# A cross-attention and expert kernel whose first tile phase takes the rows of five rounds in place of six

## The chip, the cores and the metric

One Trainium2 chip, one of its cores. The metric is the time of one execution on the device in microseconds (us); lower is better.

## The reference

The input x is 32 batches of 128 tokens with 128 features. First comes cross-attention with 16 heads of 8 features, then a layer of experts in which each token goes to its top 2 of 8:

```python
x = x + xattn(layernorm(x), ctx)          # q = x Wq', k and v = ctx Wkv', softmax over 128 keys, Wc'
xf = layernorm(x)
logits = xf @ router_w.T                  # 8 experts
top_vals, top_idx = top_k(logits, 2)
probs = softmax(top_vals)
for e in range(8):
    w = sum(where(top_idx == e, probs, 0))
    h = gelu(xf @ w1[e].T + b1[e])        # 512 hidden features, exact gelu
    out += w * (h @ w2[e].T + b2[e])
x = x + out
```

The 4096 tokens give 8192 rows, one for each token and choice.

## The kernel before

The program has two parts. The first is attention with routing, in slots s = 0 to 36; the second is a loop over 71 tiles of 128 rows.

**Attention.** In slot s the engines work on different steps of different batches. TensorE (PE) makes the scores of batch s, whose maxima DVE takes (`take_max`), and the exponent scores of batch s-3; ACT takes the exponentials; PE attends, transposes and projects batches s-4 and s-5. From slot 32 on there is no new batch, and the slots are shorter. `normalise` is DVE's step on which the transposes of a batch wait.

**Routing.** Four batches make a round; there are eight rounds, r = 0 to 7. Round r is routed in slots 9+4r and after (`routing(s, lag)`): DVE finds the two experts of each token (`top_of`, `mark_equal`, `mark_number`, `first_number`, `choose`, `pick`), sums them (`sum_round`, `carry_on`), PE makes the ranks (`rank`), and DVE turns these into row numbers (`row_ranks`, `row_terms`, `row_numbers`, `row_indices`). The two shares of a token come from the gap of its logits: POOL scales it (`scale_gap`), ACT or POOL takes the exponential (`share_ratio`), DVE finishes (`share_sum`, `share_first`, `share_second`). The normalised rows are made from POOL's `row_scale` and copied for the second choice (`copy_rows`). Then POOL sends them: `send_next` issues one indirect DMA for one batch and one choice, 128 rows, to a table in DRAM (`dispatch_d`) that has a region for each expert. A round has eight sends. Rounds 0 to 4 are sent in the slots by the plan `SENDS` (one, two, three and two sends, four to seven slots after the round begins), where `pace` may hold a send back until the exponentials are that far; round 5 by `SENDS_LAST` in the last three slots; round 6 after the last slot, in one go; round 7, which `route_last` routes on DVE after the last slot, between tiles 8 and 29, every third tile. Three buffers hold the rounds' rows.

**The table.** A tile needs the number of its expert and its first row. DVE works these out on one partition, in chains of small operations that each wait for the one before (`link`). `table_first` (three parts, in slots 33, 34 and 35) does it for the first `FIRST` = 40 tiles, which are filled from rounds 0 to 5 alone (6 x 4 x 128 x 2 rows are 48 tiles, less one for each expert's remainder); `table_second` (ten parts, behind tiles 6 to 15) for the other 31, when all counts are known. The engines load eight tiles' values into registers at a time (`table_values`, at tiles 8, 16 and so on).

**Tiles.** SP loads the expert's w1 (`load_w1`, ring of 6) and the rows (`load_tile`, ring of 12, which waits for the store of the tile 12 earlier). PE transposes the rows (`turn_tile`), ACT copies them (`copy_xg`), PE makes the hidden layer (`up`, line 1235), DVE adds the bias (`add_bias`, line 1768), ACT applies gelu, PE makes the output (`down`, line 1244), DVE adds the bias (`sum_y`), ACT multiplies by the share (`gate_y`), and POOL stores the rows by an indirect DMA (`store_tile`, lines 791 and 792). On each engine `between(t)` puts the late routing work behind the work of tile t. SP waits for the sends of rounds 3 to 5 before tile 0 and for those of rounds 5 to 7 before tile 40; it holds back w1 and rows alike. From tile 58 on ACT loads results of the first six rounds back (`load_found`), DVE adds them to x, and SP stores the output.

```python
            sp.wait_ge(sexp_done, UNITS * FIRST_BATCHES)
            for r in range(FIRST_ROUNDS - RR, FIRST_ROUNDS):
                rows_gone(sp, r)
```

Of the kernel before, what the change touches and what calls it, by code (L numbers as in the profile page):

```python
# [16 lines left out]
P = 128  # L17
# [28 lines left out]
SENDS_LAST = {0: 3, 1: 3, 2: 2}  # L46
# [6 lines left out]
FIRST_ROUNDS = 6  # L53
FIRST_BATCHES = FIRST_ROUNDS * GB
FIRST = FIRST_BATCHES * SEQ * TOPK // P - EXPERTS
REST = TILES - FIRST
OLD_TILES = FIRST + EXPERTS + 7
FIRST_GROUPS = FIRST_BATCHES // GB
# [5 lines left out]
PADS_AT = 24  # L64
LAST_SENDS_AT = 8
# [12 lines left out]
TABLE_STEPS = FIRST_STEPS + 30  # L78
# [14 lines left out]
def xattn_ffn(nc, x, ctx_t, mask, mask_t, wq_t, wkv_t, wc_t, router_t, w1_t, b1, w2_t, b2, out):  # L93
    stack = ExitStack()
    with stack:
# [77 lines left out]
        tile_no_i = sb("tile_no_i", [1, FIRST], I32)  # L173
# [18 lines left out]
        def carve(region):  # L192
            at = [0]

            def take(words):
# [9 lines left out]
        lone = carve(take(2 * TOKENS // P + FIRST + 2 * TILES + 8 * EXPERTS + 2 * EXPERTS * (TOKENS // P) + 12 * EXPERTS + 1  # L205
                          + 2 * max(FIRST * EXPERTS, REST * 2 * EXPERTS) + 2 * FIRST)[0:1])
        tile_lim, tile_no = lone(2 * TOKENS // P), lone(FIRST)
# [9 lines left out]
        expert_f, start_f = lone(FIRST), lone(FIRST)  # L217
# [14 lines left out]
        first_total_ps, total_ps = feed[:, GT - EXPERTS:GT], tail[:, GT - EXPERTS:GT]  # L232
        rank_ps = [(tail if r == ROUND - 1 else feed)[:, 0:GB * EXPERTS] for r in range(ROUND)]
# [180 lines left out]
        def _(sp):  # L414
# [115 lines left out]
            sp.wait_ge(sexp_done, UNITS * FIRST_BATCHES)  # L530
# [42 lines left out]
        def _(pool):  # L573
# [76 lines left out]
            def constants():  # L650
# [4 lines left out]
                nc.gpsimd.iota(tile_no_i[:], [[1, FIRST]], base=0, channel_multiplier=0).then_inc(iotas_made, 1)  # L655
# [69 lines left out]
            for s in range(LAST_SLOT + 1):  # L725
# [27 lines left out]
                if r is not None:  # L753
                    scale_gap(r)
                    if r >= FIRST_ROUNDS:
                        share_ratio(r)
                n = 0
                for lag, count in SENDS.items():
                    r = routing(s, 3 + lag)
                    if r is not None and r < FIRST_ROUNDS - 1:  # L760
                        for _ in range(count):
                            n += 1
                            if n > 1:
                                pace(s, n)
                            send_next(r)
                if s - LAST_SLOT + len(SENDS_LAST) > 0:
                    for _ in range(SENDS_LAST[s - LAST_SLOT + len(SENDS_LAST) - 1]):
                        send_next(FIRST_ROUNDS - 1)
# [35 lines left out]
        def _(act):  # L804
# [113 lines left out]
            for s in range(LAST_SLOT + 1):  # L918
# [43 lines left out]
                if r is not None and r < FIRST_ROUNDS:  # L962
                    share_ratio(r)
# [49 lines left out]
        def _(pe):  # L1013
# [139 lines left out]
            for s in range(LAST_SLOT + 1):  # L1153
# [19 lines left out]
                if r is not None:  # L1173
# [5 lines left out]
                    elif r == FIRST_ROUNDS - 1:  # L1179
                        pe.wait_ge(v_copied, GROUPS)  # L1180
# [97 lines left out]
        def _(dve):  # L1278
# [234 lines left out]
            def table_first(part):  # L1513
# [16 lines left out]
                if part == 2:  # L1530
                    link(nc.vector.tensor_scalar(steps_at[:, 0:EXPERTS], whole, -float(P), float(REGION), ALU.mult, ALU.add))
                    link(nc.vector.tensor_tensor(first(passed), spread(tile_no, EXPERTS), by_tile(ends[1][:, 0:EXPERTS], FIRST), ALU.is_ge))
                    link(nc.vector.tensor_reduce(expert_f, first(passed), AX.X, ALU.add))
                    link(nc.vector.tensor_copy(expert_of[:, 0:FIRST], expert_f))
                    link(nc.vector.tensor_tensor(first(passed2), first(passed), by_tile(steps_at[:, 0:EXPERTS], FIRST), ALU.mult))
                    link(nc.vector.tensor_reduce(start_f, first(passed2), AX.X, ALU.add))
# [297 lines left out]
```

## Time and profile before

| what | value |
|---|---|
| time, median of 3 runs | 385.14 us |
| time, lowest and highest | 384.53, 386.89 us |
| span of the profiled execution, first to last instruction | 383.3 us |
| busy: PE, DVE, ACT, POOL | 81%, 67%, 61%, 63% of the span |
| DMA, mean over the span | 164 GB/s |

The profiled execution is shown by its span; its own time outside the profiler's span isn't given. The median of the runs is 1.8 us above the span. Busy shares are means over stages that differ: attention runs to about 212 us, the tiles from about 221 to 370, and the last results after that.

### The profile page before, as it was taken

The page shows a single profiled execution, that of the slowest core. Times are in us where ns is not written, and L with a number is a line of the kernel's source. Part 1 is how long each engine was busy: PE and PEld are TensorE (multiplying, and loading weights), DVE is VectorE, ACT ScalarE, POOL GpSimd, SP SyncE. Part 2 cuts the span into 40 slices and gives each one's busy share as a digit, 9 for nine tenths or more (in the row PEclk, how much of TensorE's full clock was granted, in tenths as well). Part 3 has the DMA queues.
Part 4 walks back from the last instruction along what each step waited for, and adds up shares of the span by engine and source line. Part 5 has one row for each costly group of instructions (what it writes and reads, how often), then busy time and mean ns, then how long its engine had stood idle before and what let it go on. Part 6 is the DMA issues. An engine that isn't in the chain of part 4 may idle for free.

```text
span 383.3 us, 11559 instructions
## 1 busy us (share of the span) xinstructions
PE 309.2 (81%) x3720; PEld 251.8 (66%) x3720; DVE 255.3 (67%) x750; ACT 232.6 (61%) x566; POOL 241.7 (63%) x387
## 2 busy tenths in 40 slices
PE   1633878998997979797988089999999999999930
PEld 0211546666666657475765079889999999998930
DVE  7406678889788889788868826785545554556752
ACT  1311366879787878877788037556666666666520
POOL 7796335352487786858486786577877666665550
PEclk9999989999999999999999559999999999999995
DMA  5589454566474463442110386575986766669846
GB/s 152 93 212 232 130 138 114 145 111 175 124 201 129 146 170 101 130 130 58 36 54 31 96 262 185 167 223 163 275 239 196 232 202 208 204 172 353 271 119 192
DMA packets 61850, 62.95 MB, mean 164 GB/s; under 512 B 14109, under 2 KB 46260, under 8 KB 61632
## 3 DMA queue, kind: packets, MB, share of 16 engines
q1 hardware_dynamic: 55168, 50.34, 48.6%
q0 software_dynamic: 4320, 8.47, 6.4%
q10 hardware_dynamic: 2304, 3.41, 2.8%
q8 instruction: 32, 0.52, 0.6%
q14 instruction: 26, 0.21, 0.2%
HBM read 37.65 MB, written 11.88 MB: 129 GB/s over the span
## 4 chain that ended last, share of the span: by engine, by line
PE 45%; POOL 21%; issue 14%; DVE 7%; DMA 5%; SPq 4%; ACT 2%; DVEq 0%; POOLq 0%; ACTq 0%
PE sexp L1244 16%; PE smax L1235 15%; POOL dispatch_d L706 10%; PE smax L1040 3%; SPq L443 3%; DVE shift L1315 2%; PE tail L1084 2%; POOL rstd L666 2%; POOL qpart L619 2%; DMA stacks<-result_d 1%; DMA kmask<-mask_dram 1%; POOL shift L626 1%; PE feed L1031 1%; PE feed L1016 1%; POOL xq L614 1%
## 5 line engine op out<-in xcount | busy, mean ns | idle before, releaser
L1315 DVE TENSOR_REDUCE shift<-smax 128x4 f32<-128x512 f32 x128 | 87.0, 684 | 35.8 <-PE smax L1040 34.8
L792 POOL DMA_INDIRECT result_d<-y_out,stacks x71 | 70.7, 995 | 31.3 <-issue 29.5
L706 POOL DMA_INDIRECT dispatch_d<-rows_out,row_i x64 | 63.5, 993 | 34.2 <-DVE rows_out L1444 16.8
L871 ACT ACTIVATE probs<-sexp 128x512 f32<-128x512 f32 x128 | 74.2, 592 | 10.1 <-PE sexp L1048 9.1
L1235 PE MATMUL smax<-probs,w_ring 128*128 128x128 f32 x568 | 77.8, 281 | 1.6 <-ACT probs L978 1.0
L1244 PE MATMUL sexp<-w_sb,probs 128*128 x568 | 77.0, 279 | 2.6 <-ACT probs L982 2.4
L1768 DVE TENSOR_TENSOR probs<-smax,b_cols 128x512 f32<-128x512 f32 x71 | 49.1, 691 | 42.4 <-PE smax L1235 38.5
L1244 PEld LDWEIGHTS sexp<-w_sb,probs 128*128 128x128 f32 x568 | 69.8, 194 | 5.0 <-issue 4.9
L1235 PEld LDWEIGHTS smax<-probs,w_ring 128*128 128x128 f32 x568 | 70.7, 196 | 3.3 <-issue 2.9
L982 ACT ACTIVATE probs<-probs 128x512 f32<-128x512 f32 x71 | 44.8, 631 | 37.6 <-DVE probs L1768 37.5
L1040 PE MATMUL smax<-stacks 64*128 64x128 bf16 x512 | 47.9, 225 | 12.9 <-DMA stacks<-kpart 7.0
L1040 PEld LDWEIGHTS smax<-stacks 64*128 64x128 bf16 x512 | 29.3, 97 | 36.6 <-DVE shift L1315 16.6
L1048 PE MATMUL sexp<-stacks 64*128 64x128 bf16 x512 | 45.9, 219 | 0.0
L1775 DVE TENSOR_TENSOR probs<-sexp,b_sb 128x128 f32<-128x128 f32 x71 | 20.6, 291 | 21.8 <-PE sexp L1244 21.8
L1084 PE MATMUL tail<-probs,values 128*32 128x128 f32 x1024 | 34.6, 276 | 0.3 <-ACT probs L871 0.3
L987 ACT ACTIVATE y_out<-probs,stacks 128x128 f32<-128x128 f32 x71 | 28.3, 399 | 4.2 <-DVE probs L1775 4.1
L1048 PEld LDWEIGHTS sexp<-stacks 64*128 64x128 bf16 x512 | 28.0, 94 | 0.9 <-issue 0.2
L626 POOL TENSOR_TENSOR shift<-shift 128x16 f32<-128x16 f32 x32 | 7.0, 218 | 33.8 <-DVE shift L1315 33.4
L1084 PEld LDWEIGHTS tail<-probs,values 128*32 128x32 f32 x1024 | 26.0, 109 | 3.3 <-ACT probs L871 0.5
L791 POOL TENSOR_TENSOR wait_taker<-zero 128x1 f32<-128x1 f32 x71 | 14.2, 200 | 14.5 <-ACT y_out L987 14.0
L978 ACT ACTIVATE probs<-prep 128x128 f32<-128x128 f32 x36 | 9.9, 275 | 16.6 <-PE prep L1226 16.6
L1226 PE MATMUL prep<-ident_wide,stacks 128*128 128x128 f32 x36 | 10.1, 282 | 9.1 <-DMA stacks<-dispatch_d 9.1
(215 smaller groups left out, 511.4 us busy)
## 6 DMA issues: line engine op xcount, KB each, us to landing
w_ring<-w_t_dram SPq DMA_DIRECT2D x71, 256.0 KB, 3.6
stacks<-kpart SPq DMA_DIRECT2D x48, 128.0 KB
stacks<-qpart SPq DMA_DIRECT2D x48, 128.0 KB
stacks<-dispatch_d SPq DMA_DIRECT2D x71, 65.0 KB, 3.5
stacks<-result_d ACTq DMA_DIRECT2D x12, 256.0 KB, 4.4
ctx<-ctx_t_dram SPq DMA_DIRECT2D x8, 256.0 KB, 3.7
w_sb<-w_t_dram SPq DMA_DIRECT2D x8, 256.0 KB, 3.4
out_dram<-xw SPq DMA_DIRECT2D x8, 256.0 KB, 3.3
```

Source lines behind the costliest of these rows:

```text
L706: nc.gpsimd.indirect_dma_start(out=dispatch_d, out_offset=bass.IndirectOffsetOnAxis(ap=row_i[r % RR][:, k, b:b + 1], axis=0), in_=rows_out ...
L792: nc.gpsimd.indirect_dma_start(out=result_d, out_offset=bass.IndirectOffsetOnAxis(ap=xg[r][:, D + 1:D + 2].bitcast(U32), axis=0), in_=y_ou ...
L871: nc.scalar.activation(dst, sexp[hp][:], ACT.Exp).then_inc(exp_done, 1)
L982: nc.scalar.activation(hidden[i], biased[i], ACT.Gelu).then_inc(gelu_done, 1)
L987: nc.scalar.activation(y_out[r][:], y_sum[i], ACT.Copy, scale=xg[r][:, D:D + 1]).then_inc(y_gated, 1)
L1040: return nc.tensor.matmul(smax[hp][:, i, :], qstack[g][rows, 4 * m + i, ks], kstack[g][rows, 4 * m + i, ks], start=True, stop=True)
L1048: return nc.tensor.matmul(sexp[hp][:, i, :], kstack[g][rows, 4 * m + i, ks], qstack[g][rows, 4 * m + i, ks], start=True, stop=True)
L1084: last = nc.tensor.matmul(tail[32 * j:32 * (j + 1), c * SEQ:(c + 1) * SEQ], values[n // GB % 2][:, n % GB, h, :], probs[n % 2][:, h * SEQ: ...
L1235: last = nc.tensor.matmul(up_ps[i][:, c * P:(c + 1) * P], w1_ring[t % WRING][:, c * P:(c + 1) * P], xg_t[i], start=True, stop=True)
L1244: last = nc.tensor.matmul(down_ps[i], hidden[i][:, c * P:(c + 1) * P], w2_sb[:].rearrange("p e c d -> p (e c d)")[:, bass.ds(e * FF + c * ...
L1315: nc.vector.tensor_reduce(shift4[n % 2][:, hp, 0, 4 * m:4 * m + 4], smax[hp][:], AX.X, ALU.max, negate=True).then_inc(max_taken, 1)
L1768: nc.vector.tensor_tensor(biased[i].rearrange("p (c t) -> p c t", c=FC), up_ps[i].rearrange("p (c t) -> p c t", c=FC), bias, ALU.add).then ...
```

## The change

The first phase of tiles takes the rows of five rounds: `FIRST_ROUNDS` is 5 and `FIRST` 32. The constants `OLD_ROUNDS` and `OLD_BATCHES` keep the value of six for what still depends on it (the tiles below 55, and the results that ACT loads early). The first table is made two slots earlier, in slots 31 to 33, and PE's total for it in slot 30. Round 5 is now sent by `SENDS`, in slots 33 to 36. Round 6 is sent twice before the tiles and then once behind each of tiles 0 to 5; round 7 behind tiles 9, 11 and so on to 23. `route_last` is cut into three pieces behind tiles 0, 1 and 2, and the steps after it move with it: rows at tile 3, ranks at 5, row numbers at 6, shares at 7, POOL's gap and ratio at tile 3. The second table now serves 39 tiles; it also needs the tiles filled by six rounds, from a second total (`old_total_ps`), and has eleven parts, behind tiles 8 to 18. The pads go out from tile 16.

```diff
-SENDS_LAST = {0: 3, 1: 3, 2: 2}
-FIRST_ROUNDS = 6
+FIRST_ROUNDS = 5
+OLD_ROUNDS = 6
-PADS_AT = 24
-LAST_SENDS_AT = 8
+PADS_AT = 16
+SENDS_BEFORE = 2
+LAST_SENDS_AT = 9
+TABLE_AT = 8
...
 # SP, before tile 0
-            sp.wait_ge(sexp_done, UNITS * FIRST_BATCHES)
+            sp.wait_ge(sexp_done, UNITS * OLD_BATCHES)
...
 # POOL
-                    if r is not None and r < FIRST_ROUNDS - 1:
+                    if r is not None and r < OLD_ROUNDS:
                         for _ in range(count):
...
-                if s - LAST_SLOT + len(SENDS_LAST) > 0:
-                    for _ in range(SENDS_LAST[s - LAST_SLOT + len(SENDS_LAST) - 1]):
-                        send_next(FIRST_ROUNDS - 1)
...
-            for _ in range(TOPK * GB):
-                send_next(FIRST_ROUNDS)
+            for _ in range(SENDS_BEFORE):
+                send_next(ROUND - 2)
             row_scale(ROUND - 1)
             place_rows(ROUND - 1)
-            scale_gap(ROUND - 1)
-            share_ratio(ROUND - 1)
             def between(t):
-                n, off = divmod(t - LAST_SENDS_AT, 3)
+                if t < TOPK * GB - SENDS_BEFORE:
+                    send_next(ROUND - 2)
+                if t == 3:
+                    scale_gap(ROUND - 1)
+                    share_ratio(ROUND - 1)
+                n, off = divmod(t - LAST_SENDS_AT, 2)
                 if off == 0 and 0 <= n < TOPK * GB:
                     send_next(ROUND - 1)
...
 # PE, rank of a round in its slot
                     if r == FIRST_ROUNDS:
                         pe.wait_ge(table_steps, 1)
-                    elif r == FIRST_ROUNDS - 1:
-                        pe.wait_ge(v_copied, GROUPS)
+                    elif r > FIRST_ROUNDS:
+                        routed(pe, r - 1, RANKS_STEP)
...
-                if s == ROUTE_AT + GB * FIRST_ROUNDS:
+                if s == ROUTE_AT + GB * FIRST_ROUNDS + 1:
                     pe.wait_ge(carried, FIRST_ROUNDS)
-                    routed(pe, FIRST_ROUNDS - 1, RANKS_STEP)
+                    pe.wait_ge(v_copied, GROUPS)
...
 # PE, between(t)
-                if t == 1:
+                if t == 4:
                     rank(ROUND - 1)
-                if t == 4:
+                if t == TABLE_AT - 1:
                     pe.wait_ge(carried, ROUND)
                     routed(pe, ROUND - 1, RANKS_STEP)
+                    nc.tensor.matmul(old_total_ps, ones_b[:], carry[:, OLD_ROUNDS, :], start=True, stop=True)
...
 # DVE
-                late = r is not None and r < FIRST_ROUNDS - 1
+                late = r is not None and r < OLD_ROUNDS
...
-                if s == LAST_SLOT - 4:
-                    dve.wait_ge(sexp_done, UNITS * FIRST_BATCHES)
+                if s == BATCH - 2:
+                    dve.wait_ge(sexp_done, UNITS * OLD_BATCHES)
...
-                if LAST_SLOT - 3 <= s < LAST_SLOT:
-                    table_first(s - LAST_SLOT + 3)
+                if BATCH - 1 <= s < BATCH + 2:
+                    table_first(s - BATCH + 1)
...
             def between(t):
                 r = ROUND - 1
-                if t == 1:
+                if t < 3:
+                    route_last(r, t)
+                if t == 3:
                     norm_rows(r)
-                if t == 2:
+                if t == 5:
                     row_ranks(r)
                     row_terms(r)
-                if t == 3:
+                if t == 6:
                     row_numbers(r)
                     row_indices(r)
-                if t == 4:
+                if t == 7:
                     share_sum(r)
                     share_first(r)
                     share_second(r)
-                if 6 <= t < 16:
-                    table_second(t - 6)
+                if 0 <= t - TABLE_AT < 11:
+                    table_second(t - TABLE_AT)
...
-            route_last(ROUND - 1)
```

## Rows read from the trace of the kernel before

**Rows 1.** Chain that ended last, around the seam (start us, us, what).
```profile
215.22 3.15 DMA dispatch_d<-rows_out,row_i
...
218.95 1.92 DMA stacks<-dispatch_d
```

**Rows 2.** Two stretches: us, busy (x count) by engine, TensorE clock, DMA share, GB/s.
```profile
211.00:212.00 1.00, 0.80 (x4) 0.53 (x4) 0.92 (x3) 0.11 (x2) 1.00 (x1) 0.83 0.20 67
...
228.50:229.00 0.50, 0.50 (x9) 0.50 (x8) 0.17 (x1) 0.00 (x0) 0.42 (x4) 0.77 0.73 233
```

**Rows 3.** Timeline of PE: start us, us, engine, line, operation.
```profile
211.47 0.47 PE L1115 MATMUL prep<-wc_wide,y_t 128*128 128x136 f32 x2
...
228.66 1.17 PE L1235 MATMUL smax<-probs,w_ring 128*128 128x128 f32 x8
...
289.61 1.06 PE L1235 MATMUL smax<-probs,w_ring 128*128 128x128 f32 x8
```

**Rows 4.** Timeline of DVE, attention's last slots and the seam.
```profile
199.70 0.66 DVE L1432 TENSOR_SCALAR index<-ratio 128x4 f32<-128x4 f32 x1
...
201.35 0.30 DVE L1330 BATCH_NORM_STATS2 stats<-xw 128x6 f32<-128x128 f32 x1
...
203.11 0.26 DVE L1320 RECIPROCAL denom<-heads 128x16 f32<-128x16 f32 x1 [0.69 <-PE heads L1100]
...
207.12 0.15 DVE L1510 COPY stacks<-stacks 1x2 f32<-1x2 f32 x1
...
208.53 0.16 DVE L1529 SCALAR_TENSOR_TENSOR stacks<-stacks 1x8 f32<-1x8 f32 x1
...
215.34 0.28 DVE L1330 BATCH_NORM_STATS2 stats<-xw 128x6 f32<-128x128 f32 x1
...
219.17 0.17 DVE L1402 TENSOR_TENSOR carry<-carry,round_sum 128x8 bf16<-128x8 bf16 x1
```

**Rows 5.** Timeline of POOL from round 5's sends to the first store.
```profile
204.35 1.05 POOL L706 DMA_INDIRECT dispatch_d<-rows_out,row_i  x1 [0.61 <-issue]
...
216.20 0.64 POOL L683 COPY rows_out<-rows_out 128x512 f32<-128x512 f32 x1
217.64 0.99 POOL L706 DMA_INDIRECT dispatch_d<-rows_out,row_i  x1 [0.81 <-POOL rows_out L683]
...
227.48 1.05 POOL L666 TENSOR_TENSOR rstd<-var_eps,minus_half 128x4 f32<-128x4 f32 x1
...
229.03 0.19 POOL L689 TENSOR_TENSOR scaled_gap<-gap,rstd 128x4 f32<-128x4 f32 x1
...
230.27 0.19 POOL L791 TENSOR_TENSOR wait_taker<-zero 128x1 f32<-128x1 f32 x1
```

**Rows 6.** Timeline of POOL in the tile phase, and its last send.
```profile
261.37 0.96 POOL L706 DMA_INDIRECT dispatch_d<-rows_out,row_i  x1 [0.30 <-issue]
...
263.73 0.23 POOL L791 TENSOR_TENSOR wait_taker<-zero 128x1 f32<-128x1 f32 x1
264.43 0.99 POOL L792 DMA_INDIRECT result_d<-y_out,stacks  x1 [0.47 <-issue]
...
291.20 0.96 POOL L706 DMA_INDIRECT dispatch_d<-rows_out,row_i  x1 [0.30 <-issue]
```

**Rows 7.** Timeline of SP's queue: the first loads after its wait at tile 40.
```profile
297.56 0.33 SPq L520 DMA_DIRECT2D w_ring<-w_t_dram  x1
298.07 0.33 SPq L514 DMA_DIRECT2D stacks<-dispatch_d  x1
```

**Rows 8.** DMA issues on the page: operation, count, KB, median us to landing.
```profile
w_ring<-w_t_dram SPq DMA_DIRECT2D x71, 256.0 KB, 3.6
...
stacks<-dispatch_d SPq DMA_DIRECT2D x71, 65.0 KB, 3.5
```

**Rows 9.** A DVE table operation and the POOL send beside it, by timeline.
```profile
254.20 0.66 DVE L1741 TENSOR_TENSOR stacks<-stacks 1x496 f32<-1x496 f32 x1
...
254.29 1.41 POOL L706 DMA_INDIRECT dispatch_d<-rows_out,row_i  x1 [0.30 <-ACT y_out L987]
```

More of the change, by code:

```diff
@@ L77 @@
 PADS_STEP = FIRST_STEPS + 2
-TABLE_STEPS = FIRST_STEPS + 30
+TABLE_STEPS = FIRST_STEPS + 33
 def bf16_parts(value):
@@ L232, in xattn_ffn @@
         first_total_ps, total_ps = feed[:, GT - EXPERTS:GT], tail[:, GT - EXPERTS:GT]
+        old_total_ps = tail[:, GT - 2 * EXPERTS:GT - EXPERTS]
         rank_ps = [(tail if r == ROUND - 1 else feed)[:, 0:GB * EXPERTS] for r in range(ROUND)]
@@ L961, in _ @@
                 r = routing(s, 3)
-                if r is not None and r < FIRST_ROUNDS:
+                if r is not None and r < OLD_ROUNDS:
                     share_ratio(r)
@@ L1635, in _ @@
                     row_numbers(r)
-                if r is not None and r >= FIRST_ROUNDS - 1:
+                if r is not None and r >= OLD_ROUNDS:
                     row_indices(r)
@@ L1656, in _, with route_last @@
                         row_moments(3)
-            def route_last(r):
-                row_stats2(BATCH - 1)
-                top_of(r, 0)
-                row_moments2(BATCH - 1)
-                mark_equal(r, 0)
-                row_var2(r)
-                mark_number(r, 0)
-                first_number(r, 0)
-                choose(r, 0)
-                mask_first(r)
-                top_of(r, 1)
-                mark_equal(r, 1)
-                mark_number(r, 1)
-                first_number(r, 1)
-                choose(r, 1)
-                pick(r)
-                top_gap(r)
-                sum_round(r)
-                carry_on(r)
+            def route_last(r, part):
+                if part == 0:
+                    row_stats2(BATCH - 1)
+                    top_of(r, 0)
+                    row_moments2(BATCH - 1)
+                    mark_equal(r, 0)
+                    row_var2(r)
+                    mark_number(r, 0)
+                if part == 1:
+                    first_number(r, 0)
+                    choose(r, 0)
+                    mask_first(r)
+                    top_of(r, 1)
+                    mark_equal(r, 1)
+                    mark_number(r, 1)
+                if part == 2:
+                    first_number(r, 1)
+                    choose(r, 1)
+                    pick(r)
+                    top_gap(r)
+                    sum_round(r)
+                    carry_on(r)
             def between(t):
                 r = ROUND - 1
-                if t == 1:
+                if t < 3:
+                    route_last(r, t)
+                if t == 3:
                     norm_rows(r)
-                if t == 2:
+                if t == 5:
                     row_ranks(r)
                     row_terms(r)
-                if t == 3:
+                if t == 6:
                     row_numbers(r)
                     row_indices(r)
-                if t == 4:
+                if t == 7:
                     share_sum(r)
@@ L1712, in table_second @@
                     link(nc.vector.tensor_tensor(count, last_row[0:1, :], first_row[0:1, :], ALU.subtract))
-                if part == 1:
+                if part in (1, 2):
+                    if part == 2:
+                        link(nc.vector.tensor_copy(count, old_total_ps[0:1, :]))
                     link(nc.vector.tensor_tensor(over[:, :, 0, :], spread(count, TOKENS // P),
@@ L1716, in table_second @@
                                                  ALU.is_gt))
-                    link(nc.vector.tensor_reduce(ceil_new, over[:, :, 0, :], AX.X, ALU.add))
+                    link(nc.vector.tensor_reduce((ceil_new, floor_ceil[:, :, 0])[part - 1], over[:, :, 0, :], AX.X, ALU.add))
+                if part == 3:
                     link(nc.vector.tensor_tensor(tiles_of[:, 0:EXPERTS], floor_ceil[:, :, 0], done, ALU.subtract))
-                if part == 2:
                     link(nc.vector.tensor_tensor(tiles_of[:, EXPERTS:], ceil_new, floor_ceil[:, :, 0], ALU.subtract))
@@ L1724, in table_second @@
                                                         in1=first_row[0:1, :], op0=ALU.mult, op1=ALU.add))
-                if part == 3:
+                if part == 4:
                     link(nc.vector.memset(first_at[:, 2 * EXPERTS:], float(EXPERTS * REGION)))
```

45 lines of the change are left out of this document (23 added, 22 removed).

## The prediction

> **What bounds the kernel now.** I read the chain that ended last first. At the seam between attention and tiles it runs through POOL's sends of round 5, the landing of the last one (215.22 + 3.15 = 218.37) and the load of tile 0 (218.95, landed 220.87) [rows 1]. The timeline of PE shows what waits on it: attention's last matmul ends at 211.94, and tile 2's up matmuls start only at 228.66 [rows 3]. The table of stretches adds that TensorE's granted clock falls from 2.4 to 1.2 GHz inside 211 to 212 us, after slots in which PE was partly idle, and is back within 228.5 to 229.0 [rows 2]. From tile 2 to tile 32 PE takes 60.95 us, 2.03 per tile, with DVE's table work in it [rows 3]; from there on the chain is nearly all PE. So a gain must come from the seam, and every later wait of PE counts against it. The change pays for an earlier start with a nearer second deadline: the last round's rows must have landed before tile 32, where they now have until tile 40.
>
> **The seam.** Tile 0 now needs rounds 0 to 4 only, whose sends go out in slots 29 to 32, before the first row of round 5's here (204.35) [rows 5]. What is late next is the table. Its first part on DVE moves from slot 33's end to slot 31's; DVE idles there for normalise, and PE's rank of round 5, which now waits for the first table step, still comes before the shift it would wait for anyway, so I cost slot 31 at nothing. In slot 32 round 5's share work and two constants (199.70 to 201.35, 1.65) leave and the second part (207.12 to 208.69, 1.57) comes in. In slot 33 DVE worked 1.07 us, 201.35 to 202.42, and idled 0.69 before normalise at 203.11 [rows 4]; with the share work, about 1.0 more, round 5's shares are ready at about 203.3 and normalise slips by 0.4 at most. Slots 34 and 35 lose two parts; attention ends at 211.9 plus or minus 1.
> The last table part then ends at about 206.7 (normalise 203.6 to 204.1, and about 2.6, an estimate: it is the longest part). SP needs at most 5.4 us from there to the load (derived below), so tile 0 lands between 212.3 and 214.0. Before, 7.8 us passed from the landing at 220.87 [rows 1] to 228.66, at half clock and with route_last off DVE's path. With the clock fallen likewise, tile 2 starts at 211.9 + 0.3 + 7.8 = 220.0, against 228.66: 8.7 us earlier. If the clock stays up some 2 us more is won; that is one end, the later landing (+1.8) the other. I take the row that exists: half clock.
>
> **DVE after the seam.** route_last (215.34 to 219.34, 4.0 us) [rows 4] goes in three pieces of 1.2 to 1.5 behind tiles 0, 1 and 2. The first lies in the start-up and is free; the others exceed what DVE has free in a tile by 0.2 to 0.5 each, less at half clock. The table of the rest grows: two more operations for the old total, eleven parts for ten, 624 elements for 496 in the four operations over tiles (0.66 each [rows 9], so 0.17 more each), and its longest part now falls in tile 16, where DVE also reloads its registers. I put all this at 1.5 us of PE's time, between 0.5 and 3. The new wait is at tile 7: share_sum of the last round waits for POOL's ratio, with add_bias of tile 8 queued behind it, and PE's down behind that. Tile 8 comes at 220.0 + 6 x 2.03 = 232.2; POOL makes the ratio at about 234.3 (next part); so 1 to 2 us. PE's own path to tile 32: 220.0 + 60.95 + 1.5 + 1.5 = 283.9.
>
> **POOL and the second deadline.** This is the term that decides. Before, from 204.35 POOL works without a break to 216.84: eight sends, place_rows, gap, ratio, copy_rows, 12.49 us [rows 5]. Now the first send can go at 203.6 (shares at 203.3), and row_scale with its offset, which used POOL's idle before, lies inside: 1.3 plus a gap of 0.2, so 203.6 + 12.5 + 1.5 = 217.6. As before, 0.8 pass to round 6's first send: 218.4. Eight of them took 9.84 (217.64 to 227.48), so two take 2.5; row_scale and place_rows 1.55 (227.48 to 229.03) [rows 5]: store 0 at 222.4, where before it was at 230.27. Its tile would have allowed it some 3 us earlier: POOL starts in debt.
> Then six pairs of store and send, each 263.73 - (261.37 - 0.30) = 2.66 [rows 6], 16.0; gap and ratio at tile 3, 1.24 (229.03 to 230.27) [rows 5]; stores 6 to 8 at 2.66 - 1.26 = 1.40, 4.2; seven times two stores and a send, 4.06, 28.4; store 23 and the last send, 2.66. Sum: 222.4 + 16.0 + 1.2 + 4.2 + 28.4 + 2.7 = 274.9 for the end of the last send. PE gives POOL 2.03 per tile, so the debt is hardly paid off before tile 24, and POOL sets this time, not PE.
> Before, the last send ended at 292.16 and SP issued the first load behind its wait at 297.56 [rows 6, 7]: 5.4 us for landing and two register loads. So 280.3 for w1 and 280.8 for the tile; they land 3.6 and 3.5 later in the median [rows 8], 1.9 in an empty queue [rows 1]: 283.9 and 282.7 to 284.3. With about 0.8 for turn and copy tile 32's matmuls start between 283.9 and 285.1, where PE could have started at 283.9. Two chains that end so close, both uncertain, give a little more than either: 284.7. Before it was 289.61 [rows 3]. So of 8.7 us 4.9 are left.
>
> A busy time of POOL would have given another answer: 0.96 for a send where the spacing is 1.26. The Trainium skill (Perfetto Trace Analysis, GPSIMD Instruction) says to time GpSimd by the start-to-start spacing of its instructions and not by the reported duration. The rows agree, with a gap of 0.30 before the send; by durations the fourteen sends behind store 0 alone would come out 4.2 us shorter.
>
> **The rest.** The number of tiles is 71 in both, the register reloads fall on the same tiles, the result loads still begin at tile 58, the tail is the same. Pads go out at tiles 16 to 23 in place of 24 to 31, beside POOL's debt: load 16 waits for store 4, at about 236, landed near 240, and is due at tile 15's transpose, near 247. No cost. The span of 383.3 would become 378.4. The profiled execution is shown by its span alone; the median of the runs is 1.8 above it, which I keep: 385.14 - 4.9 = 380.2.
>
> **Rivals.**
> 1. POOL doesn't bind: the shares come earlier, or its debt is repaid while PE waits on DVE, so that tile 32 finds its rows. For it: PE's own waits at tiles 7 and 16 give POOL time. Against it: POOL is in debt from store 0 on. PE's path alone is 283.9, without the wait at tile 7 282.3, with full clock 280.3: gains of 5.7 to 9.3, 376 to 379.5. Chance 0.15.
> 2. POOL falls further behind, and the change turns slower. Mechanism: a store that follows a store doesn't always take 1.40; at 264.43 a gap of 0.47 stood in it [rows 6], 0.31 more than the 0.16 which the pair has. On 24 stores that is 7.4 us: last send 282.3, tile 32 at about 291.5 to 292.1, 2 us later than before, 387.3. It decides from 4.9 us of additional POOL time on. Against it: the gap stood there once where POOL was behind, and is usual only where it waits. Chance 0.06.
> 3. DVE and POOL get in each other's way. One send took 1.41 in place of 0.96, beside a DVE operation with two inputs of SBUF [rows 9]. If all fourteen sends behind store 0 did, it is 14 x 0.45 = 6.3 us, 1.4 more than the gain: 386.5. The change puts six of them beside route_last. Seven of the eight in the tiles before did not show it, so one or two of these is in my range. Chance 0.05.
> The Trainium skill (SBUF — State Buffer, Who interferes with whom) has such a rule: a DVE instruction with two SBUF inputs holds the read port that GpSimd needs, and one in a 2-port mode both, for the whole instruction. By that rule sends and stores beside the last round's work would be late as in rival 3; the one row agrees, the others leave it open.
> 4. PE's path is longer than mine: the wait at tile 7 spreads (POOL makes the ratio later) and the pieces of route_last each stop PE. Up to 3 us on top: tile 32 at 287 to 288, 383. Chance 0.14.
>
> **How the numbers follow.** The forecast, 378.3 to 382.3 around 380.2, has 0.60; rival 1 0.15, rival 4 0.14, rivals 2 and 3 together 0.11. A measurement of this kernel can tell about 1% from no change, 3.85 us: faster means below 381.3, slower above 389.0. Of the forecast's own chance 0.43 lies below 381.3, with rival 1 0.58, and a little of rival 4: 0.60. Slower by over 1% needs 4 us more than rivals 2 and 3 give in the mean: 0.05. The rest is 0.35. The range runs from 377 (half of rival 1 left out) to 385 (rivals 2 and 3 left out).
>
> **What would show it.** Right: tile 0's load lands near 213 and tile 2 starts near 220; the clock falls near 212 as before; the first send of round 5 near 203.6; store 0 near 222.4; the last send ends near 275 at store 23, with no gap between POOL's stores and sends until then; SP's queue is empty for some microseconds before tile 32, and PE idles there for 1 to 3 us; DVE waits at tile 7 for the ratio. Wrong: a PE wait of 5 us or more at tile 32, a wait for a y_sent before it, tile 2 later than 222, or no wait at tile 32 at all.

## The result and the profile after

The changed kernel takes 392.6 us (median of 4 runs, 391.9 to 394.5) where the kernel before takes 384.9 beside it: ratio 1.0202, 95% interval 1.0165 to 1.0238. The forecast was 380.2, in a range from 377 to 385. The change makes the kernel 2% slower. Every ratio below leaves out single executions that ran slower than the others of their kernel, so it needn't be the quotient of the two medians. The span of the profiled execution is 390.2 us, against 383.3.

The page of the changed kernel: span, busy time, and the chain that ended last.

```profile
span 390.2 us, 11564 instructions
...
PE 309.4 (79%) x3721; PEld 252.5 (65%) x3721; DVE 254.5 (65%) x753; ACT 231.7 (59%) x566; POOL 243.3 (62%) x387
...
PE 37%; POOL 24%; issue 17%; DVE 8%; SPq 4%; DVEq 4%; DMA 3%; ACT 2%; POOLq 0%; ACTq 0%
```

PE is busy as long as before (309 us) and stands still for 7 us more. New in the chain is DVEq, 4% of the span, where the kernel before had 0%: DVE's sequencer, doing something that is no computation. The seam first, since that was the aim. Timelines of PE and POOL of the changed kernel, to be read against [rows 3] and [rows 5]:

```profile
213.93 0.45 PE L1230 MATMUL prep<-ident_wide,stacks 128*128 128x128 f32 x1 [3.62 <-DMA stacks<-dispatch_d]
216.30 2.05 PE L1239 MATMUL smax<-probs,w_ring 128*128 128x128 f32 x8 [1.93 <-issue]
...
221.95 1.06 PE L1239 MATMUL smax<-probs,w_ring 128*128 128x128 f32 x8
...
288.81 1.06 PE L1239 MATMUL smax<-probs,w_ring 128*128 128x128 f32 x8
...
293.22 1.13 PE L1239 MATMUL smax<-probs,w_ring 128*128 128x128 f32 x8 [1.44 <-issue]
```

```profile
202.01 0.99 POOL L710 DMA_INDIRECT dispatch_d<-rows_out,row_i  x1 [2.24 <-DVE rows_out L1449]
...
223.07 0.19 POOL L795 TENSOR_TENSOR wait_taker<-zero 128x1 f32<-128x1 f32 x1 [1.51 <-ACT y_out L991]
...
278.36 0.97 POOL L710 DMA_INDIRECT dispatch_d<-rows_out,row_i  x1 [0.30 <-issue]
```

Tile 2 starts at 221.95, 6.7 us earlier than before. Tile 32 starts at 288.81, 0.8 earlier. After that the kernel only loses. PE's first matmuls on tile 0 show the sign of the cause: 1.93 us between the turned tile and them, with nothing in the profile that released them. What the sequencers do there stands in the rows of line 409, `table_values`, which reads eight tiles' numbers from SBUF into registers. First the changed kernel (engine, operation, count, then shortest, median and longest in ns), then the kernel before, where the same line is 405:

```profile
L409 SPq TENSOR_LOAD <-stacks x18: 1467/1712/1947, 204.6 to 347.0; - x18
L409 DVEq TENSOR_LOAD <-stacks x9: 1658/1881/2181, 212.7 to 357.0; - x9
L409 PEldq TENSOR_LOAD <-stacks x9: 1957/2028/2592, 213.9 to 358.6; - x9
```

```profile
L405 SPq TENSOR_LOAD <-stacks x18: 522/1227/1802, 213.3 to 341.0; - x18
L405 DVEq TENSOR_LOAD <-stacks x9: 594/604/1058, 219.2 to 351.6; - x9
L405 PEldq TENSOR_LOAD <-stacks x9: 587/632/1072, 221.0 to 353.1; - x9
```

There are as many loads as before, of the same size, at the same tiles, and each takes in the median 1.88 us on DVE where it took 0.60, and 2.03 on PE where it took 0.63. (These rows carry a q behind the engine's name: the profile doesn't count them as busy, and most views leave them out.) The chain of the changed kernel shows that they aren't hidden; at tile 24 and at tile 32:

```profile
272.31 0.29 DVE probs L1787
272.60 1.74 DVEq L409
...
274.56 0.70 DVE probs L1780
...
275.39 1.13 PE smax L1239 x8
...
289.41 1.61 DVEq L409
...
291.24 0.70 DVE probs L1780
```

DVE finishes a tile, reads its registers, and only then adds the bias that frees the buffer in which PE makes a later tile. The start of `add_bias` by DVE's timeline gives the sum of it:

| add_bias of tile | before | changed | difference |
|---|---|---|---|
| 2 | 230.06 | 223.77 | -6.3 |
| 32 | 290.81 | 291.24 | +0.4 |
| 39 | 304.26 | 305.87 | +1.6 |
| 40 | 306.15 | 308.98 | +2.8 |
| 58 | 341.07 | 346.49 | +5.4 |
| 70, the last | 365.61 | 372.94 | +7.3 |

From tile 39 to 70, where the two programs do the same work, the changed kernel still loses 5.7 us, and it loses nearly all of them at tiles 40, 48, 56 and 64, where the registers are read again.

**What the change did to these loads.** The table of experts, `expert_of`, lies in one long row of 4-byte words, in the buffer `stacks`, behind the row `tile_no`. (The extract of the diff in The change leaves this edit out.) In the kernel before `tile_no` has `FIRST` = 40 words; in the changed one `MOST` = max(32, 39) = 39. So `expert_of` starts at word 9855 of `stacks` in place of 9856, and each group of eight starts at an odd word in place of a multiple of eight. `start_of`, which lies 71 words on and which only SP reads, was at an odd word before as well: SP's 18 loads, nine from each row, run from 0.52 to 1.80 us in the kernel before and from 1.47 to 1.95 in the changed one, where both rows start off. Theory A: the start of the eight words makes the load slow, and this is the whole loss. Theory B: the load is slower for another reason (what runs beside it, other rows, the later place in the program), or the loss is in the new order of work and the loads are only seen with it.

### The profile page after: what moved, and what is told of

Its sections match the earlier page's. It is cut to its first block, busy times and chain, and to the rows that moved or that the text cites. A ratio compares the mean times of both kernels' runs of the same rounds, so it can differ in the third digit from the quotient of the medians.

```text
span 390.2 us, 11564 instructions
## 1 busy us (share of the span) xinstructions
PE 309.4 (79%) x3721; PEld 252.5 (65%) x3721; DVE 254.5 (65%) x753; ACT 231.7 (59%) x566; POOL 243.3 (62%) x387
## 4 chain that ended last, share of the span: by engine, by line
PE 37%; POOL 24%; issue 17%; DVE 8%; SPq 4%; DVEq 4%; DMA 3%; ACT 2%; POOLq 0%; ACTq 0%
PE sexp L1248 12%; POOL dispatch_d L710 11%; PE smax L1239 11%; DVEq L409 3%; PE smax L1044 3%; SPq L447 3%; DVE probs L1780 2%; DVE shift L1320 2%; POOL rstd L670 2%; PE tail L1088 2%; POOL qpart L623 1%; POOL shift L630 1%; DMA stacks<-result_d 1%; DMA kmask<-mask_dram 1%; PE feed L1035 1%
## 5 line engine op out<-in xcount | busy, mean ns | idle before, releaser
L796 POOL DMA_INDIRECT result_d<-y_out,stacks x71 | 71.5, 1006 | 28.5 <-issue 26.6
L795 POOL TENSOR_TENSOR wait_taker<-zero 128x1 f32<-128x1 f32 x71 | 15.2, 214 | 23.0 <-ACT y_out L991 22.6
L1770 DVE TENSOR_TENSOR xw<-xw,stacks 128x512 f32<-128x512 f32 x16 | 11.0, 689 | 7.4 <-DMA stacks<-result_d 7.0
```

What stands on the lines that cost most here:

```text
L796: nc.gpsimd.indirect_dma_start(out=result_d, out_offset=bass.IndirectOffsetOnAxis(ap=xg[r][:, D + 1:D + 2].bitcast(U32), axis=0), in_=y_ou ...
```

## The experiments

Seventeen runs were made, of ten kernels, in six series, each beside the kernel before. (The expectations say "call" for a series.) In four of the series (e1 to e4, e5 to e8, e9 and e10, e11 and e12) every kernel, the kernel before included, took 8 to 10% longer than beside the changed kernel above: PE, ACT and DVE stood still for 1 to 4 us at a time, with no releaser in the profile, in attention and in the tiles; in the tiles at much the same places in e10, e11 and e12. In the last two (e13 to e15, e16 and e17) the kernel before took 384.6 and 384.8 us again. So times are compared by ratios and differences inside one series, and the absolute sum is judged by the last two. Traces of different series are compared only where the kernel before took the same to about 1% in both.

**e1_aligned, e5_aligned_again: the change, with one unused word.**

```diff
         tile_lim, tile_no = lone(2 * TOKENS // P), lone(MOST)
+        lone(1)
```

> The kernel after, with one unused word between tile_no and expert_of, so that the tile table starts again at a multiple of 16 words, as in the kernel before. Theory A (a register load of 8 words is slow when its first word isn't at a multiple of 8 words; the change moved the table by one word, 40 to 39): loads of PE and DVE fall from 2.03 and 1.88 to about 0.63 and 0.60 us, eight reloads in the tiles cost PE about 1.4 us less each, time 381 +- 2, near the forecast. Theory B (the loads are slow because of the new program: its code, its size, or traffic beside them): loads and time stay, 392. Theory C (both): in between.

> The kernel of e1 again, since in its call every kernel ran some 10% longer than in the first runs, that of before too (422 us). Theory A, now that e1 showed the loads back at 0.6 us: 381 +- 2, ratio to before 0.98 to 0.995. Theory B: 392, ratio 1.02.

Measured: 426.8 us, ratio 1.0163 (1.0078 to 1.0248), and 426.2, ratio 1.0166 (1.0078 to 1.0253). The loads are 606 and 610 ns (DVE, PE), and 600 and 620. One word brings them back. Whether the time follows can't be read from these two alone, since the changed kernel wasn't in their series.

**e2_before_shifted, e7_before_shifted_again: the kernel before, with the same unused word.**

```diff
         tile_lim, tile_no = lone(2 * TOKENS // P), lone(FIRST)
+        lone(1)
```

> The kernel before, with one unused word ahead of the table and nothing else. Theory A: loads of PE and DVE rise to about 2.0 and 1.9 us, time 385 + 8 x 1.4 = 396 +- 2. Theory B: no change, 385.

> The kernel of e2 again. Theory A: 396 +- 2, ratio 1.025 to 1.035. Theory B: 385.

Measured: 435.2 us, ratio 1.0371 (1.0304 to 1.0439), and 432.4, 1.0335 (1.0208 to 1.0463). Loads of 1886 and 1875 ns on DVE, 2032 and 2017 on PE. The rows of e2:

```profile
L406 DVEq TENSOR_LOAD <-stacks x9: 1671/1886/2422, 243.6 to 395.4; - x9
L406 PEldq TENSOR_LOAD <-stacks x9: 1951/2032/2393, 246.4 to 396.9; - x9
```

This is the cause alone, with nothing of the change: one word costs 3.3 to 3.7% by the ratios, 10 to 13 us between the medians given.

**e3_both_rows_aligned, e6_both_rows_again, e4_before_start_aligned: the second table as well.**

```diff
-        expert_of, start_of = (lone(TILES).bitcast(I32) for _ in range(2))
+        expert_of, start_of = (lone(TILES + 1)[:, 0:TILES].bitcast(I32) for _ in range(2))
```

> As e1, and one more word so that start_of, which SP alone loads, starts at a multiple of 8 words too. Theory A: SP's loads of it fall from 1.7 to about 0.53 us as well; SP's way from the last send to the load of tile 32 gets 1.2 us shorter. If POOL's last send is what binds (the forecast), e3 is 1 to 1.2 us below e1; if PE's own path or nothing there binds, e3 equals e1.

> The kernel of e3 again. If POOL's last send binds at tile 32: 1.2 us below e5. If nothing binds there: equal to e5.

> The kernel before with start_of at a multiple of 8 words. Theory A: SP's loads of it fall from 1.77 to 0.53 us, but before tile 0 SP waits for round 5's rows after its loads, and at tile 40 its rows come in time: 385, within 0.5.

Measured: e3 424.4 us beside 422.5 (no ratio is on record for it); e6 425.0, ratio 1.0103 (1.0016 to 1.0191); e4, which is the kernel before with this edit, 419.6, 0.9964 (0.9914 to 1.0015). SP's loads fall from 1213 to 524 ns, 526 and 530 in the median: SP too has slow loads only where they start off. In the kernel before it is worth nothing that can be told. e3 and e6 are 2.4 and 1.2 us under e1 and e5 by the medians, which these runs can't tell from nothing either.

**e8_before_shifted_by_4, e15_before_shifted_by_2: which start is wanted.** Four and two unused words in the kernel before.

> The kernel before with four unused words ahead of the table, so that expert_of starts at a multiple of 4 words but not of 8. If a load is slow whenever its eight words aren't in one aligned block of 8, it is as slow as in e7 (2.0 and 1.9 us, 396). If a multiple of 4 words is enough, 0.6 us and 385.

> The kernel before with two unused words in front of the table, so that the rows of eight values start at an even word that is no multiple of four. A shift by one gave loads of 1.88 us on DVE and 2.0 on PE, a shift by four 0.60 and 0.63. If a multiple of two is enough 0.6 here and the time of before; if a multiple of four is wanted 1.9, and about 10 us more.

Measured: by four words, 423.3 us beside 422.2, ratio 1.0059 (1.0001 to 1.0116), loads of 601 and 632 ns in the median (one of PE's nine took 1.88 us). By two words, 399.1 us in one run beside 384.6, 3.8% more. Its loads:

```profile
L406 DVEq TENSOR_LOAD <-stacks x9: 1628/1891/2240, 218.3 to 364.9; - x9
L406 PEldq TENSOR_LOAD <-stacks x9: 1952/2018/2438, 221.6 to 366.5; - x9
```

A multiple of four words (16 bytes) is fast; one word or two behind it is slow alike, with the program otherwise as it was.

**e9_after_itself, e10_aligned_third: the change and the aligned change in one series.**

> The kernel after, unchanged, for a comparison inside one call with the aligned one. Theory A: ratio to before 1.02 in a call like the first; 10 to 12 us above e10. Theory B: equal to e10.

> The kernel after with the table back at a multiple of 16 words (as e1 and e5). Theory A: 10 to 12 us below e9; in a call like the first 381. Theory B: equal to e9.

Measured: 430.7 us, ratio 1.0331 (1.0268 to 1.0395), and 422.2, 1.013 (1.0065 to 1.0195). In one series the word is worth 8.4 us. That is most of the 10 to 12 that theory A had given, and against theory B; but in this kind of series the aligned change is still slower than the kernel before.

**e11_aligned_fourth, e12_aligned_seam_held: is the earlier start worth its length?** e12 lets SP wait for round 5's sends before tile 0, as the kernel before does.

```diff
-            for r in range(FIRST_ROUNDS - RR, FIRST_ROUNDS):
+            for r in range(FIRST_ROUNDS - RR, FIRST_ROUNDS + 1):
                 rows_gone(sp, r)
```

> The changed kernel with one unused word more, so that the table of experts starts at a multiple of 16 words, as before. Theory A (only the slow register loads are wrong in the change): in a call in which the kernel before takes about 385 us, 381 (ratio 0.99). Where the kernel before takes about 420 us, because PE stands still at regular places in every kernel, the three runs of this kernel so far gave 1.013 to 1.017 of it; theory B (there the 9 us by which the tiles start earlier are lost to PE's stalls in tiles 3 to 28) gives the same again.

> As the run beside it, but SP's wait before tile 0 is for round 5's rows too, as in the kernel before: the load of tile 0 waits for the last of these sends (issued near 215, landed near 219 in a profile of 390 us), some 6 to 7 us later than in the change. All else stays. If the earlier start is worth what its length says (theory A), this is 4 to 7 us slower than the run beside it (POOL's stores, and with them the sends of round 7 and tile 32, move by as much). Theory B, in a call in which the kernel before takes about 420 us: 0 to 2 us slower, and PE's stalls in tiles 3 to 28 (15 us and more in sum of single waits without a releaser) shrink by 4 to 6 us.

Measured: e11 425.7 us, 1.018 (1.0077 to 1.0283); e12 427.4, 1.0209 (1.0124 to 1.0294). In their profiles tile 2's `add_bias` comes at 244.57 and 248.76, the last at 401.64 and 405.56, and from tile 2 to 32 both take the same, 80.9 and 80.4 us. Not all of the 4.2 us between the starts is the edit: by PE's timeline attention ended at 235.7 in e11, at 237.3 in e12 and at 239.0 in e10, which is the kernel of e11 in another series. So the edit held tile 2 back by 2.5 us, not by the 6 to 7 expected. The distance is still there at the end (3.9), though the medians, 1.8 apart, can't tell it. The tiles from 2 to 32 didn't shrink by more than e10 and e11 differ (79.9 and 80.9). That speaks against the idea that the early start only feeds the pauses, but so small a shift doesn't rule it out. The aligned change has more of the pauses: 80.9 us for tiles 2 to 32, where e4, the order of before, takes 68.4. The costliest in e11, on PE:

```profile
279.63 1.06 PE L1249 MATMUL sexp<-w_sb,probs 128*128 x8
284.30 2.05 PE L1240 MATMUL smax<-probs,w_ring 128*128 128x128 f32 x8 [3.61 <-issue]
```

PE stands 3.61 us and comes back at the lower clock (1.2 GHz granted from 284.3 to 288.0; 2.05 us for eight matmuls that take 1.06 elsewhere). What stops the engines in such series isn't shown by any view that was read.

**e13_aligned_fifth: the aligned change in a series like the first.**

> The changed kernel with one unused word more once again, beside the next run. If the kernel before takes about 385 us in this call, theory A (the slow register loads are all that is wrong) says 381 to 384. If it takes about 420 us, theory A has no price; the four calls so far gave 1.013 to 1.018 of the kernel before, and this should again.

Measured: 380.8 us (378.5 to 382.8) beside 384.6, ratio 0.9894 (0.9829 to 0.9959). The prediction's sum has no term for slow loads, and for this kernel its result holds, in part by luck, as the next section shows. Its loads, and its timelines of PE, DVE and POOL:

```profile
L410 SPq TENSOR_LOAD <-stacks x18: 522/1223/1777, 206.6 to 337.5; - x18
L410 DVEq TENSOR_LOAD <-stacks x9: 594/611/1061, 214.7 to 348.0; - x9
L410 PEldq TENSOR_LOAD <-stacks x9: 590/609/1078, 214.8 to 349.7; - x9
```

```profile
214.75 0.45 PE L1231 MATMUL prep<-ident_wide,stacks 128*128 128x128 f32 x1 [2.43 <-DMA stacks<-dispatch_d]
215.71 2.05 PE L1240 MATMUL smax<-probs,w_ring 128*128 128x128 f32 x8 [0.51 <-ACT probs L983]
...
285.34 1.06 PE L1240 MATMUL smax<-probs,w_ring 128*128 128x128 f32 x8
286.87 0.33 PE L1231 MATMUL heads<-ident_wide,stacks 128*128 128x128 f32 x1 [0.47 <-DMA stacks<-dispatch_d]
```

```profile
235.00 0.17 DVE L1438 TENSOR_SCALAR index<-ratio 128x4 f32<-128x4 f32 x1 [0.94 <-POOL ratio L699]
...
251.74 0.80 DVE L1751 TENSOR_TENSOR stacks<-stacks 1x624 f32<-1x624 f32 x1
...
255.01 0.80 DVE L1754 TENSOR_TENSOR stacks<-stacks 1x624 f32<-1x624 f32 x1
```

```profile
204.03 0.99 POOL L711 DMA_INDIRECT dispatch_d<-rows_out,row_i  x1 [2.23 <-DVE rows_out L1450]
...
222.47 0.20 POOL L796 TENSOR_TENSOR wait_taker<-zero 128x1 f32<-128x1 f32 x1 [0.46 <-ACT y_out L992]
...
251.83 1.59 POOL L797 DMA_INDIRECT result_d<-y_out,stacks  x1 [0.16 <-issue]
...
255.12 1.53 POOL L711 DMA_INDIRECT dispatch_d<-rows_out,row_i  x1 [0.31 <-ACT y_out L992]
...
276.00 0.97 POOL L711 DMA_INDIRECT dispatch_d<-rows_out,row_i  x1 [0.30 <-ACT y_out L992]
```

**e14_aligned_route_last_whole: DVE's last routing in one piece.**

```diff
-                if t < 3:
-                    route_last(r, t)
...
+            for part in range(3):
+                route_last(ROUND - 1, part)
             dve.wait_ge(bias_loaded, 32)
```

> As the run beside it, with all three pieces of route_last before tile 0, as in the kernel before. Where the slots of tiles 2 to 31 are 12 us longer than the same tiles of the kernel before, theory C says that DVE's work between the tiles is what stretches them: then these tiles shrink by 2 us or more, and as route_last takes 4.0 us of which 3 lie in the start-up, the time falls or stays. Theory D: the pieces cost what the sum said (under 1 us), and the stretched slots lie at tiles 3, 5, 8, 12, 14 to 16 as before: the time is 0 to 2 us longer, since add_bias of tile 0 waits for the whole of route_last.

Measured in the series of e13: 383.2 us, ratio 0.9949 (0.9914 to 0.9983), against 0.9894 (0.9829 to 0.9959); the intervals overlap, and the two profiled spans are 380.1 and 380.0. Cutting the routing in pieces is worth between nothing and 2.4 us. That fits theory D. Theory C couldn't be tried as it was meant, since the series had no stretched tiles.

**e16_both_rows_third, e17_both_rows_and_w1_first: the chain to tile 32.** e16 is e3 again. e17 in addition:

```diff
                 if t == FIRST:
                     sp.wait_ge(table_steps, TABLE_STEPS)
-                    for r in range(ROUND - RR, ROUND):
-                        rows_gone(sp, r)
-                    sp.wait_ge(pads_sent, 16 * EXPERTS)
-                    sp.wait_ge(idle_rows_stored, 16)
...
                     load_w1(t, t % WRING, experts[in_bulk(t)])
+                if t == FIRST:
+                    for r in range(ROUND - RR, ROUND):
+                        rows_gone(sp, r)
+                    sp.wait_ge(pads_sent, 16 * EXPERTS)
+                    sp.wait_ge(idle_rows_stored, 16)
                 load_tile(t, t % TRING, starts[in_bulk(t)])
```

> The changed kernel with the row of experts and that of first rows both on a multiple of 16 words (one unused word before them, one behind each). In the profile of the change with only the first row so placed, SP's two register loads at tile 32 take 0.56 and 1.75 us after the last send has landed, and the loads of tile 32 follow them (281.02, 281.54); with both rows placed the second should take 0.53, so tile 32 about 1.2 us earlier: in a call with the kernel before at about 385 us, 379 to 380 (0.986). Rival: PE's own path (283.9 at tile 32 by the prediction) takes over and less than 0.5 is won. In a call with the kernel before at about 420, where PE doesn't wait at tile 32, nothing is won over the aligned change (1.010 to 1.018).

> As the run beside it; in addition SP reads its registers for tile 32 and issues this tile's w1 before it waits for the sends, and only the rows (and all behind them) wait. If the chain from the last send over SP to tile 32 sets the time there, the load of the rows goes out 1.6 us earlier (two register loads and one issue, 0.53 each) and the time falls by up to that; if PE's own path does by now, it stays within 0.5. About 378.5 to 379.5 in a call with the kernel before at 385.

Measured: 378.6 us, ratio 0.9837 (0.9793 to 0.988), and 377.6, 0.9803 (0.9756 to 0.985), beside 384.8. The chain of e13 ahead of tile 32:

```profile
276.00 2.29 DMA dispatch_d<-rows_out,row_i
...
278.50 0.56 SPq L410
...
279.09 1.75 SPq L410
...
281.02 0.33 SPq L525
```

The last send lands 2.29 us after its issue, and SP's two register loads, one fast and one slow, stand between that and the first load for tile 32. In e16 the same loads go out as follows (SP's queue, then PE around tile 32):

```profile
277.94 0.33 SPq L525 DMA_DIRECT2D w_ring<-w_t_dram  x1
278.45 0.33 SPq L519 DMA_DIRECT2D stacks<-dispatch_d  x1
```

```profile
282.29 1.06 PE L1249 MATMUL sexp<-w_sb,probs 128*128 x8
283.18 1.06 PE L1240 MATMUL smax<-probs,w_ring 128*128 128x128 f32 x8
284.07 0.27 PE L1231 MATMUL heads<-ident_wide,stacks 128*128 128x128 f32 x1
```

PE goes through tile 32 without a wait, and its chain there is PE alone. Tile 33's `add_bias` follows tile 32's after 2.13 us (3.01 in e13), tile 32's follows tile 31's after 1.89 (3.03). So in e13 the chain from the last send did set the time, as forecast, and was worth 2 us of waits at tiles 32 and 33. In e16 the first load goes out 3.1 us earlier than in e13. Only 1.2 of these are the faster load at tile 32. The last send itself ends 1.9 us earlier (275.08): the second slow load of SP stood before tile 0 as well, so tile 2's `add_bias` comes 1.4 us earlier (221.76, 223.17), and one operation of POOL fewer is slowed by DVE. The row `start_of` is thus paid for at the seam and at tile 32. Now PE's own path sets the time, and in e17 the rows go out early for nothing more: from tile 2 to tile 32 it takes 62.5 us, e16 62.6, and the 377.6 and 378.6 aren't told apart. e17 and e16 are the best kernels of this study, 1.6 to 2% under the kernel before; their gain over e13 (0.9894, another series) is at the edge of what the intervals can tell.

## Why the prediction was wrong

The result lies outside the range, with the wrong sign. The step that failed is in the paragraph "The rest": "the register reloads fall on the same tiles", with which they are put at nothing. They do fall on the same tiles. But the edit that looked emptiest, `MOST` in place of `FIRST` in the length of a row, moved what they read by one word, and each became 1.3 us longer on DVE and 1.4 on PE (medians). Between the changed kernel and e13, which differ in that word alone, `add_bias` comes later by 0.6 us at tile 2, 4.9 at tile 33, 9.0 at tile 58 and 10.5 at the end. The 0.6 hides a part: attention happened to end 2.0 us earlier in the changed kernel (210.3, 212.3; e16 and e17, the same program up to tile 32, differ by as much), so the slow loads before tile 0 cost 2.6. Seven of the eight reloads in the tiles cost 1.2 to 1.5 each; the one at tile 32 costs 0.4, as it lies beside the wait for the rows. I had counted the loads and not asked what sets the time of one, although the trace of before held the warning: SP's loads, equal but for the row that they read, took from 0.52 to 1.80 us. Of the signs of being wrong that the prediction lists one came true in the changed kernel, no wait of PE at tile 32: PE was late by then for the other reason. Tile 2, at 221.95, stayed just under the 222.

The other terms, against e13, which differs from the changed kernel in that word alone:

| step | forecast | changed kernel | e13, aligned |
|---|---|---|---|
| attention ends | 211.9, 1 either way | 210.3 | 212.3 |
| first send of round 5 | 203.6 | 202.01 | 204.03 |
| tile 0's rows are there | 212.3 to 214.0 | 213.9 | 214.8 |
| tile 2 starts | 220.0 | 221.95 | 221.36 |
| POOL turns to store 0 | 222.4 | 223.07 | 222.47 |
| DVE waits at tile 7 for the ratio | 1 to 2 | 0.94 | 0.94 |
| last send ends | 274.9 | 279.33 | 276.97 |
| first load for tile 32 | 280.3 | 284.53 | 281.02 |
| tile 32 starts | 284.7 | 288.81 | 285.34 |
| time | 380.2 | 392.6 | 380.8 |

- **The seam.** Right in mechanism, 1.4 us too good for tile 2: the gain is 7.3, not 8.7. The 220.0 needs the rows at 212.2; they were there at 214.75, 0.8 after the late end of my bracket. SP issued their load early enough (210.89, where the sum has up to 212.1), but PE could start on them only 3.9 us later, where 2.05 passed before (218.95 to 221.00 by PE's timeline). What made the load slow isn't shown; before, the first w1 loads went out 3.0 us ahead of it, now 1.6. Of the 2.5 us by which the rows were late 1.1 came back: from the rows to tile 2 it was 6.6 us and not 7.7, as the lower clock ended sooner. It fell later too, inside 212 to 214 (0.50 from 213 on) and not inside 211 to 212 as in [rows 2]. Stretches of e13 (us, busy time of PE, PEld, DVE, ACT, POOL, clock, DMA):

```profile
211.00:212.00 1.00, 0.41 (x3) 0.41 (x4) 0.50 (x3) 0.54 (x2) 0.70 (x2) 1.00 0.88 309
212.00:213.00 1.00, 0.32 (x3) 0.12 (x2) 0.00 (x0) 0.28 (x1) 0.98 (x2) 0.92 0.95 307
...
219.00:221.00 2.00, 1.89 (x13) 1.66 (x13) 1.08 (x6) 1.50 (x3) 1.67 (x3) 0.83 0.74 227
```

PE waits for tile 0 from 212.3 on, and its first eight matmuls of a tile take 2.05 us, twice the 1.06 of the full clock; by 221 the 2.4 GHz are back (granted 0.67 in 219 to 220, 1.00 from 220 on).

- **PE's own path to tile 32.** 60.75 us of `add_bias` between tiles 2 and 32 before, 63.4 in e13. That is 2.7 more, of which 1.1 is the wait for tile 32's rows; forecast 3.0 for the table work and the wait at tile 7 together.
- **POOL's chain.** The term that I called decisive decided: POOL works from store 0 to the last send with hardly a gap, the end is on e13's chain, store 0 is right to 0.1 us, and the last send ends 2.1 us later than my sum. 1.2 of these are two operations of 1.59 and 1.53 us in place of 1.0, each beside a DVE operation of 0.80 us with two inputs from SBUF; most of the rest are gaps of 0.54 and 0.23 us in the first two stores and one `wait_taker` of 0.50. That is rival 3 in small: it hit two of POOL's operations, not fourteen. The Trainium skill's rule (SBUF — State Buffer, Who interferes with whom), that a DVE instruction with two SBUF inputs keeps GpSimd from its read port, agrees with these rows, and with [rows 9]. In all three the operation of POOL began 0.1 us behind that of DVE; where a send began 0.01 us behind one (e16, 253.85) or 0.17 ahead of one (e14, 255.52) it took 0.96 and 0.97, so two inputs from SBUF alone don't make it slow. The way from the end of the send to SP's first load was 4.05 us and not 5.4. These two errors, 2.1 too early and 1.4 too long, nearly cancel; that the first load of tile 32 came within 0.7 us of the forecast is luck.
- **Behind tile 32.** I let the gain stand from there on. Tile 33's rows were late as well, so `add_bias` is 4.2 us ahead of before at tile 32 and 3.3 at tile 33, and stays so (3.1 at the last). The forecast kept 4.9 to the end; these 0.9 us were missing from the sum. At tile 32 itself the gain was 4.2 to 4.3 and the forecast 4.9.
- **The sum.** The median of e13, 380.8, is 0.6 us from the forecast; its profiled span, 380.0, is 1.6 from the forecast's 378.4. The span is the comparison for which the terms were added up, and its agreement rests on errors of both signs.
- **The rivals.** None of the four was the cause of the loss. Three asked how long engines work or wait on one another; only rival 3 asked whether an instruction might take another time, and it asked it of POOL's sends, not of the register loads.

For series in which every kernel is 8 to 10% slower the prediction would have had the wrong sign even for the aligned change (1.013 to 1.018). There the tiles from 2 to 32 are 12 us longer than in the order of before (e11 and e4). Why the new order meets more of those pauses stays open; the two edits tried on it (e12, and e14, which met a series without them) didn't settle it.

## What to carry to other kernels

A change of a buffer's length moves whatever is carved out behind it. Before such a change is costed at nothing, list what is read behind it by an instruction that cares about its address, above all register loads in the sequencers, and pin these rows to multiples of 16 bytes. When a kernel has two instances of one instruction with two durations, as SP's loads here, find out why before the forecast: some edit can set the higher price on all of them. And look at rows of the sequencers (the q behind the engine) as well as at busy time; this loss stands in no group of busy instructions.

## What the runs showed of the hardware

A load of eight registers from SBUF takes 0.60 us on DVE, 0.63 on PE and 0.53 on SP when the eight words start at a multiple of four words, and about 1.9, 2.0 and 1.7 when they start one, two or three words behind one (e2, e15, the changed kernel). Eight words that start at a multiple of four but not of eight are as fast (e8). The Trainium skill (DMA: Bandwidth & Descriptors, Latency and other measured facts) gives about 600 ns as the floor of such a load. The aligned ones on DVE and PE agree; those on SP, at 0.52 to 0.53, lie somewhat under it. In a chain that lets PE wait for DVE, the additional 1.3 us showed nearly in full at seven of eight reloads (1.2 to 1.5 us each, the changed kernel against e13).

The kernel before took 417 us in one series and 385 in a later one, with the same program. An experiment that has to tell an absolute forecast from a miss needs the kernel before beside it, and both kernels that it compares in one series.
